# A decoder layer's expert stage: order of the last blocks, place of a token's two expert rows, and who weighs the last two tiles

## The reference

```python
x = hidden_states.reshape(-1, H)                      # 1024 tokens, H = 256
logits = jnp.einsum('th,eh->te', x, gate_w)           # 16 experts
topk_w, topk_idx = jax.lax.top_k(_softmax(logits), 2)
combine = jnp.sum(jax.nn.one_hot(topk_idx, E) * topk_w[..., None], axis=1)
gu = jnp.einsum('th,ehj->etj', x, w_gate_up)          # I = 176, gate and up
y = jnp.einsum('eti,eih,te->th', _swiglu(gu, I), w_down, combine)
y = y + _swiglu(x @ shared_gate_up, 2 * I) @ shared_down
```

## Time and profile before

| | us |
|---|---|
| median of 3 runs | 245.59 (244.62 to 246.39) |
| profiled execution, device time | 245.34 |
| its span | 243.5 |
| around the span | 1.84 |
| TensorE busy in it | 223.9 (92%) |
| VectorE / ScalarE / GpSimd busy | 144.6 / 123.3 / 77.1 |

### The profile page before, as it was taken

How to read it: one execution, slowest core, us unless ns; L and a number is a source line. 1 busy time by engine, 2 the same in 40 slices (tenths; PEclk the granted TensorE clock), 3 DMA queues, 4 the chain that set the end, 5 groups by cost and what they waited for, 6 DMA issues and landing times.

```text
span 243.5 us, 5429 instructions
## 1 busy us (share of the span) xinstructions
PE 223.9 (92%) x1800; PEld 156.7 (64%) x1800; DVE 144.6 (59%) x442; ACT 123.3 (51%) x444; POOL 77.1 (32%) x95
## 2 busy tenths in 40 slices
PE   8978899999999999999999999999999999998970
PEld 6535566656666676889778788776555556554540
DVE  1568878888878878343989468955222322222175
ACT  2136988989898888923242520702333334333310
POOL 2221121111121101020474100274577777752330
PEclk9999999999999999999999999999999999999996
DMA  6999977500001900001502200032595323655596
GB/s 214 264 347 349 316 172 168 133 13 1 1 3 31 307 5 0 4 0 25 215 0 76 99 0 0 5 79 58 146 287 203 108 92 99 155 164 183 178 287 242
DMA packets 21662, 30.62 MB, mean 126 GB/s; under 512 B 2361, under 2 KB 17347, under 8 KB 21635
## 3 DMA queue, kind: packets, MB, share of 16 engines
q1 hardware_dynamic: 18627, 23.34, 32.5%
q0 software_dynamic: 2304, 6.29, 8.7%
q10 hardware_dynamic: 704, 0.64, 0.8%
HBM read 25.02 MB, written 5.24 MB: 124 GB/s over the span
## 4 chain that ended last, share of the span: by engine, by line
PE 56%; ACT 14%; DVE 11%; DMA 8%; issue 5%; SPq 2%; POOL 2%; DVEq 0%; ACTq 0%; POOLq 0%
PE bank L948 11%; ACT pr_s L1073 10%; PE bank L965 7%; PE bank L873 5%; PE bank L575 5%; PE bank L617 4%; PE bank L604 3%; DMA x_s<-expert_out 3%; PE bank L702 3%; PE bank L937 2%; PE bank L927 2%; DMA bxT<-in_wh_t 2%; PE bank L580 2%; PE bank L667 2%; DMA early<-in_w_gu 1%
## 5 line engine op out<-in xcount | busy, mean ns | idle before, releaser
L1073 ACT ACTIVATE pr_s<-bank,mx 128x128 f32<-128x128 f32 x128 | 45.2, 384 | 8.0 <-DVE mx L1302 8.0
L1635 DVE COPY bxT<-bank 128x256 f32<-128x256 f32 x24 | 10.1, 423 | 41.3 <-PE bank L950 38.7
L948 PE MATMUL bank<-gu_s,bxT 128*64 x96 | 31.3, 466 | 1.4 <-DMA early<-in_w_gu 1.4
L536 POOL DMA_INDIRECT expert_out<-by,prT x24 | 23.7, 987 | 17.6 <-ACT by L1063 13.6
L1063 ACT ACTIVATE prT<-bank 128x512 f32<-128x512 f32 (+1 forms) x56 | 27.4, 514 | 2.7 <-PE bank L617 1.8
L1073 ACT ACTIVATION_READ_ACCUMULATOR pr_s<-bank,mx 128x1 f32 x128 | 28.7, 224 | 0.0
L531 POOL DMA_INDIRECT qx_s<-ffn_in,prT x24 | 23.4, 976 | 16.5 <-issue 8.9
L1302 DVE TENSOR_REDUCE mx<-bank 128x4 f32<-128x512 f32 x32 | 20.5, 683 | 4.7 <-PE bank L604 4.7
L965 PE MATMUL bank<-dn_s,prT 88*64 x96 | 22.7, 379 | 0.4 <-ACT prT L1063 0.4
L617 PE MATMUL bank<-tab,pr_s 128*128 128x128 f32 x128 | 19.5, 275 | 3.1 <-ACT pr_s L1073 2.7
L873 PE MATMUL bank<-ck_s,sgu_s 128*128 128x256 f32 (+1 forms) x96 | 22.3, 382 | 0.0
(11 more groups left out here) (203 smaller groups left out, 474.1 us busy)
## 6 DMA issues: line engine op xcount, KB each, us to landing
gu_s<-in_w_gu SPq DMA_DIRECT2D x8, 704.0 KB, 7.3
dn_s<-in_w_dn SPq DMA_DIRECT2D x4, 704.0 KB
early<-in_w_gu SPq DMA_DIRECT2D x8, 352.0 KB, 5.0
early<-in_w_dn SPq DMA_DIRECT2D x8, 176.0 KB
gu_s<-in_ctx_in SPq DMA_DIRECT2D x2, 512.0 KB, 9.6
ffn_in<-x_s SPq DMA_DIRECT2D x4, 256.0 KB, 2.2
cv_s<-expert_out SPq DMA_DIRECT2D x4, 256.0 KB, 3.7
x_s<-expert_out SPq DMA_DIRECT2D x4, 256.0 KB, 5.5
```

The costliest lines, as they stand in the source:

```text
L536: pool.indirect_dma_start(expert_out[:], bass.IndirectOffsetOnAxis(ap=idx[:, 1, k:k + 1], axis=0), by[:, k % RB, :], None).then_inc(dma_sc ...
L948: mm(bank[2 + i % 2][0:HT, 0:2 * I], bxT[:, i % 2, k, 0:HT], gu_s[:, k, bass.ds(e, 1), :], start=k == 0, stop=k == KD - 1, skip_group_chec ...
L1073: last = nc.scalar.activation(pr_s[:, n % 2, h, :], score_bank(n)[:, h * T:(h + 1) * T], ACT.Exp, bias=mx[:, n % 4, h:h + 1], accum_out=de ...
```

## The change

Five edits in one version:

1. A token's two rows of `expert_out` lie side by side: row 2 x token + (0 for the best expert, 1 for the second). The index formula has the same number of operations. The reload reads `(b p k) d`, one piece of 2 KB per partition.
2. TensorE's order: `shared_up(3, 1)` moves from behind block 1's up to behind block 20's down. The loop ends at i = 20 without block 21's up; after it come hidden transpose 20, up 21, down 20, `shared_up(3, 1)`, hidden transpose 21, up 22, up 23, down 21, `shared_up(3, 2)`, hidden transposes 22 and 23, down 22, down 23. ScalarE and VectorE follow the same order. The wait of the first two `expert_down` on the last pair's c = 1 goes; block 1's waits on c = 0. Banks of c = 1 and 2 of the last pair are 6 and 7 in place of 4 and 6.
3. SP's staging order: up 0, up 1, down 0, down 1, up 2, up 3, then (up 4, up 5, down 2, down 3), (up 6, up 7, down 4, down 5), down 6, down 7 (numbers are blocks less 16); waits as before.
4. VectorE makes four diagonal 128 x 128 matrices of the weights of tiles 6 and 7 (`diagonals`, `dg`), and TensorE adds diagonal x rows to the shared expert's result in PSUM (4 matmuls of 128 x 256) once tile 6's, then tile 7's reload has landed. VectorE's `weigh_pair(6)` (4 operations) is gone; its last two additions stay.
5. VectorE does `shared_add(1)` and `shared_add(2)` ahead of `bT_out(0)`.

The diff, with its few constant declarations left out:

```diff
@@ -106,7 +106,7 @@
     c[:, R_RING + RB:R_RING + 2 * RB] = 2 * E + 2 * (RB - 1 - np.arange(RB))
-    c[:, R_DUMMY:R_DUMMY + BLOCKS] = DUMMY + T * np.arange(BLOCKS) + p + 1
+    c[:, R_DUMMY:R_DUMMY + BLOCKS] = DUMMY + T * np.arange(BLOCKS) + p + 2
     return c
@@ -197,6 +197,7 @@
         staged = early[0][:, 0:SB * (KD * 2 * I + 2 * D)].rearrange("p (r n) -> p r n", r=SB)
+        dg = early[0][:, SB * (KD * 2 * I + 2 * D):][:, 0:4 * T].rearrange("p (b k t) -> p b k t", b=2, k=2)
         gu_x = staged[:, :, 0:KD * 2 * I].rearrange("p r (k n) -> p r k n", k=KD)
@@ -336,7 +338,7 @@
         bei = sb("bei", [1, MORE], i32)
-        shared_bank = lambda q, c: bank[((6, 7, 1) if q < PAIRS - 1 else (5, 4, 6))[c]]
+        shared_bank = lambda q, c: bank[((6, 7, 1) if q < PAIRS - 1 else (5, 6, 7))[c]]
         hidden_bank = lambda i: bank[(1, 0)[i % 2]]
@@ -419,21 +421,34 @@
             sp.wait_ge(pe_expert_up, RB)
-            for j in range(BLOCKS - E):
-                e = staged_expert[j]
+            def stage_up(j):
                 if j >= SB:
                     sp.wait_ge(pe_expert_up, E + j - SB + 1)
-                sp.dma_start(gu_x[:, j % SB], w_gu[bass.ds(e, 1), :, :, :].rearrange("e p k n -> p (e k) n")).then_inc(dma_staged_up[j % SB], 16)
+                sp.dma_start(gu_x[:, j % SB], w_gu[bass.ds(staged_expert[j], 1), :, :, :].rearrange("e p k n -> p (e k) n")).then_inc(dma_staged_up[j % SB], 16)
+
+            def stage_down(j):
                 if j >= SB:
                     sp.wait_ge(pe_expert_down, E + j - SB + 1)
-                sp.dma_start(dn_x[:, j % SB], w_dn[bass.ds(e, 1), :, :, :].rearrange("e p k n -> p (e k) n")).then_inc(dma_staged_down[j % SB], 16)
+                sp.dma_start(dn_x[:, j % SB], w_dn[bass.ds(staged_expert[j], 1), :, :, :].rearrange("e p k n -> p (e k) n")).then_inc(dma_staged_down[j % SB], 16)
+
+            for j in range(0, BLOCKS - E, 2):
+                stage_up(j)
+                stage_up(j + 1)
+                if j >= SB:
+                    stage_down(j - 2)
+                    stage_down(j - 1)
+                elif j == 0:
+                    stage_down(0)
+                    stage_down(1)
+            stage_down(BLOCKS - E - 2)
+            stage_down(BLOCKS - E - 1)
             sp.wait_ge(dve_ring, 1)
...
             for t in range(B):
-                sp.dma_start(yg[t],
-                             expert_out[0:SLOTS, :].rearrange("(k b p) d -> b p k d", k=2, b=B)[t]).then_inc(dma_token_outputs[t], 16)
+                sp.dma_start(yg[t].rearrange("p k d -> p (k d)"),
+                             expert_out[0:SLOTS, :].rearrange("(b p k) d -> b p (k d)", k=2, b=B)[t]).then_inc(dma_token_outputs[t], 16)
             for t in range(B - 2):
@@ -957,8 +972,8 @@
                     pe.wait_ge(act_expert_out, i - 1)
-                if i < 2:
-                    pe.wait_ge(dve_shared_hidden, SC * (PAIRS - 1) + 2)
+                if i == 1:
+                    pe.wait_ge(dve_shared_hidden, SC * (PAIRS - 1) + 1)
                 if i >= E:
@@ -1026,38 +1041,47 @@
             expert_up(1)
-            shared_up(PAIRS - 1, 1)
             block_transpose(2)
             block_transpose(3)
-            for i in range(2, BLOCKS, 2):
+            last = BLOCKS - 1
+            for i in range(2, BLOCKS - 2, 2):
                 hidden_transpose(i - 2)
                 hidden_transpose(i - 1)
-                if i + 2 < BLOCKS:
-                    block_transpose(i + 2)
-                    block_transpose(i + 3)
+                block_transpose(i + 2)
+                block_transpose(i + 3)
                 expert_up(i)
-                if i + 2 < BLOCKS:
+                if i + 4 < BLOCKS:
                     expert_up(i + 1)
...
                 expert_down(i - 1)
-                if i + 2 < BLOCKS:
-                    read_expert(i + 2)
-                    read_expert(i + 3)
-                else:
-                    expert_up(i + 1)
+                read_expert(i + 2)
+                read_expert(i + 3)
+            hidden_transpose(last - 3)
+            expert_up(last - 2)
+            expert_down(last - 3)
+            pe.wait_ge(dve_block_T, last)
+            shared_up(PAIRS - 1, 1)
+            hidden_transpose(last - 2)
+            expert_up(last - 1)
+            expert_up(last)
+            expert_down(last - 2)
             shared_up(PAIRS - 1, 2)
-            hidden_transpose(BLOCKS - 2)
-            hidden_transpose(BLOCKS - 1)
-            expert_down(BLOCKS - 2)
-            expert_down(BLOCKS - 1)
+            hidden_transpose(last - 1)
+            hidden_transpose(last)
+            expert_down(last - 1)
+            expert_down(last)
             for c in range(SC):
...
                 for b in range(2):
-                    last = mm(last_pair_out(b), shT[0:r, (PAIRS - 1) % 2, c, b * T:(b + 1) * T], sdn_s[0:r, c, :],
-                              start=c == 0, stop=c == SC - 1)
-                    if c == SC - 1:
-                        last.then_inc(pe_shared_down, 1)
+                    mm(last_pair_out(b), shT[0:r, (PAIRS - 1) % 2, c, b * T:(b + 1) * T], sdn_s[0:r, c, :],
+                       start=c == 0, stop=False)
+            pe.wait_ge(dve_diagonals, 1)
+            for b in range(2):
+                pe.wait_ge(dma_token_outputs[B - 2 + b], 16)
+                for k in range(2):
+                    last = mm(last_pair_out(b), dg[:, b, k, :], yg[B - 2 + b][:, k, :], start=False, stop=k == 1)
+                last.then_inc(pe_shared_down, 1)
         @block.scalar
@@ -1242,21 +1266,28 @@
             silu(1)
-            shared_silu(PAIRS - 1, 1)
-            for i in range(2, BLOCKS, 2):
+            last = BLOCKS - 1
+            for i in range(2, BLOCKS - 2, 2):
                 hT_out(i - 2)
...
                 silu(i)
-                if i + 2 < BLOCKS:
+                if i + 4 < BLOCKS:
                     silu(i + 1)
...
                 y_out(i - 1)
-            silu(BLOCKS - 1)
+            hT_out(last - 3)
+            silu(last - 2)
+            y_out(last - 3)
+            shared_silu(PAIRS - 1, 1)
+            hT_out(last - 2)
+            silu(last - 1)
+            silu(last)
+            y_out(last - 2)
             shared_silu(PAIRS - 1, 2)
-            hT_out(BLOCKS - 2)
-            hT_out(BLOCKS - 1)
-            y_out(BLOCKS - 2)
-            y_out(BLOCKS - 1)
+            hT_out(last - 1)
+            hT_out(last)
+            y_out(last - 1)
+            y_out(last)
             act.wait_ge(dve_shared_added, PAIRS + 1)
@@ -1566,7 +1597,7 @@
                 link(V.reciprocal(top_w[0], s8[:, 6, :]))
-                link(V.tensor_tensor(top_w[1], second_exp, top_w[0], ALU.mult))
+                V.tensor_tensor(top_w[1], second_exp, top_w[0], ALU.mult).then_inc(dve_weights, 1)
@@ -1608,12 +1639,12 @@
             link(V.tensor_tensor(ids[:, 1, :], best_n, ids[:, 0, :], ALU.add))
-            link(V.tensor_scalar(ids[:, 2, :], ids[:, 0, :], 0.0, float(B * T), ALU.is_gt, ALU.mult))
+            link(V.tensor_scalar(ids[:, 2, :], ids[:, 0, :], 0.0, -2.0, ALU.is_gt, ALU.add))
             V.tensor_scalar(idx[:, 0, :], ids[:, 1, :], -1.0, 0.0, ALU.add, ALU.max)
...
             link(V.tensor_tensor(ids[:, 3, :], ids[:, 3, :], ids[:, 2, :], ALU.add))
-            V.scalar_tensor_tensor(idx[:, 1, :], ids[:, 3, :], -1.0, ids[:, 1, :], ALU.add, ALU.add).then_inc(dve_rows, 1)
+            V.scalar_tensor_tensor(idx[:, 1, :], ids[:, 1, :], 2.0, ids[:, 3, :], ALU.mult, ALU.add).then_inc(dve_rows, 1)
             shared_mul(2, 2)
@@ -1648,33 +1679,43 @@
+            def diagonals():
+                dve.wait_ge(dve_weights, 1)
+                for b in range(2):
+                    for k in range(2):
+                        last = V.tensor_scalar_mul(dg[:, b, k, :], idf, top_w[k][:, B - 2 + b:B - 1 + b])
+                last.then_inc(dve_diagonals, 1)
+
+            shared_add(1)
+            shared_add(2)
             bT_out(0)
-            shared_add(1)
             bT_out(1)
...
             h_mul(1)
-            shared_add(2)
-            shared_mul(PAIRS - 1, 1)
             bT_out(2)
...
             router_weights()
-            for i in range(2, BLOCKS, 2):
-                if i + 2 < BLOCKS:
-                    bT_out(i + 2)
+            diagonals()
+            last = BLOCKS - 1
+            for i in range(2, BLOCKS - 2, 2):
+                bT_out(i + 2)
                 h_mul(i)
-                if i + 2 < BLOCKS:
+                if i + 4 < BLOCKS:
                     bT_out(i + 3)
-                h_mul(i + 1)
+                    h_mul(i + 1)
+            h_mul(last - 2)
+            bT_out(last)
+            shared_mul(PAIRS - 1, 1)
+            h_mul(last - 1)
+            h_mul(last)
             shared_mul(PAIRS - 1, 2)
...
             weigh_pair(4)
-            weigh_pair(6)
             for b in range(2):
...
                 dve.wait_ge(pe_shared_down, PAIRS + b)
```

(4 more changed lines are left out.)

## The result

The changed kernel takes 242.38 us in the median of four runs (242.22 to 242.47), where the kernel before took 245.92 in four (244.62 to 246.39; the 245.59 of the table above is the median of three of them): a ratio of 0.9864, with a 95% interval of 0.9824 to 0.9904. It is faster by 1.4%, not by the 2.2% forecast. The profiled execution took 242.47 us with a span of 240.6, so 1.87 us lie around it (1.84 before); the forecast had a span of 238.05. The missing 2.5 us are all at the end, as the rows show from the front on.

A forecast was written before the change was run, and what follows sets the result against it. Bound: TensorE's program up to block 20's down, then the reloads. Last addition at 235.8, plus 2.25 gives span 238.05 (5.45 us less); 1.84 around it and 0.25 for the median give 240.1 us, range 238.6 to 242.4.

The forecast's parts named there:

- the front's gain: Loop front: without `shared_up(3, 1)` there, block 2's up begins at 168.1 to 168.4, taken as 2.0 us earlier.
- the stall for staged weights: TensorE before block 21's up: SP's new order removes the wait, a gain of 1.56 us (ends 0 and 1.56).
- block 20's down and the reloads: Loop end: block 20's down begins at 220.13 instead of 225.21, so the reloads begin at 224.28, 5.1 us earlier.
- The cover that was named: Idle time or room said to hide the `shared_add`, the making of four diagonals and the reloads' landing, each costed at nothing.
- The four diagonal matmuls are 128 x 256 like the twelve, 2.86 / 12 = 0.24 each: 0.96: TensorE's end: the diagonal products add 0.96 us, so TensorE ends at 235.1.
- 2.25 us on, the span ends: Program end: the last addition ends at 235.8 and the span 2.25 us later, at 238.05.
- rival A: Program end: a transfer, scatter 23's landing or the last stores, sets the end; span 238.7, time 240.8; chance 0.13.
- a hold of one weighing: Within rival A: a scatter's issue on GpSimd might be held by one two-input VectorE weighing, 0.5 us.
- B: Loop end: the staging stall only moves, to block 20's or 22's weights; up to 1.56 us, time 241.7; chance 0.11.
- C: Loop front: the gain is not had, a gather or something hidden holds it; 2.0 us, time 242.1; chance 0.07.
- D: Block loop: scatters of interleaved rows land late and hold `y_out`; slower, up to 248.8 us; chance 0.03.
- E: Reloads: 2 KB pieces do not shorten the landing; changes nothing in the time, no chance of its own.

The follow-up runs named there:

- three diagonals: Changed kernel with waits before weighings 6, 7, 9 and 10, and tile 6's best row weighed on VectorE again, leaving three diagonal products: 240.20 us, ratio 0.9796.
- four gaps: Changed kernel with only weighings 6, 7, 9 and 10 waiting for the one before: ratio 0.9842 on the second chip; 240.55 us, ratio 0.9807 on the third.

## Why the prediction was right and where it failed

**Right.** What bound the kernel before, and every step up to the first weighing: the front's gain of 2.0 us (168.30 in the trace), the stall for staged weights gone, block 20's down and the reloads 5.0 us sooner, each within 0.13 us. The cover that was named hid what it should: `shared_add` and the diagonals cost nothing, and the reloads of tiles 6 and 7 landed at 232.7 and 234.4, before the products of tile 6, at 234.07, and of tile 7, at about 235.0, wanted them. All this holds for the first result and the third chip; on the second the front's gain did not reach the reloads.

**Failed, the term "The four diagonal matmuls are 128 x 256 like the twelve, 2.86 / 12 = 0.24 each: 0.96".** The mechanism was right, the size half. A float32 product with 128 columns of weights leaves two records, and the "twelve" of the earlier trace rows are six instructions (three chunks, two tiles), as the eight of a `shared_up` are four; the unit should have been 0.48 us for an instruction. The products took 1.89 us, and the weighings were quicker than summed (4.8 us, not 5.6, since back to back they come every 0.40 us). Together the last addition ended 0.6 us later than forecast. The run with three diagonals confirms the term.

**Failed, the step "2.25 us on, the span ends", and with it the price of rival A.** The forecast took the stretch from the last addition to the end from the trace of before. Rival A named the scatter of block 23 as what might set the end instead, and that is what happened, but not by its landing, which took 2.5 us: by its issue, 3.0 us late. The forecast weighed a hold of one weighing, 0.5 us, and dismissed it because one scatter beside weighings had taken 0.97 us. That one had a gap of 0.11 us to get in by, and the next, of 1.05 us, was passed over. The change itself took the gaps away: with every reload landed before its own weighing is due (tile 3's at 230.5 for the sixth weighing at 231.4, tile 5's at 232.1 for the tenth at 233.0), VectorE has nothing to wait for, and the twelve weighings form one unbroken row. The held scatter took 3.85 us, and GpSimd's drain, which ended at 242.3 in the kernel before, 1 us ahead of SP, became the last. With the hold taken away alone (four gaps, third chip) the span is 238.6 us, 0.55 above the forecast of 238.05, and the last addition, at 236.35, is late by the same 0.55, which is the diagonals' part.

The page "SBUF — State Buffer" of the Trainium skill, section Who interferes with whom, says that a VectorE instruction with two SBUF inputs contends with a GpSimd instruction that reads SBUF, and that one with a single SBUF input, outside the two-port modes, does not. The runs agree with both halves: 3.85 us with two, 0.97 with one from PSUM. In its bullet on the two-port modes the page has the other engine blocked for a whole instruction. Two scatters here were held for one weighing, 1.10 and 1.19 us; the scatters of four runs were held for the whole row, 3.85 and 5.44 us.

**Luck.** The measured 242.38 us lies just inside the stated range of 238.6 to 242.4. That is chance: the upper end was there for rivals such as B and C, which did not come in this run, and the hold of 1.9 us stood in no term.

**Rivals B, C and D** did not come in the first result: no wait before block 20's down, block 2's up on time, and ScalarE waited for a scatter only once, for 1.5 us, off the path. On the first two chips of the experiments ScalarE's copies wait 19 to 28 us for an unrecorded release in every kernel traced, also with the rows in their old place. **E** was right in its effect as far as the runs can tell: the kernel before with 2 KB pieces has the ratio 0.999.

## What to carry to other kernels

A helper engine off the critical path may need gaps in its neighbour's work, and a change that packs the neighbour's instructions without gaps can starve it; when weighing such a hold, take the length of the unbroken row as its upper end, not that of one instruction. Test a change on more than one chip before its parts are priced: what binds the loop may differ. Where the end of a program moves forward, look at every engine's closing instruction, not at the last store alone, since one that ended shortly before may be next. Count matmuls as instructions, from the code, before taking a price from records.

## What the hardware showed that was not expected

- VectorE's weighings back to back start every 0.40 us though each lasts 0.47. Beside such a row with two SBUF operands a GpSimd scatter took 3.85 us (twelve weighings, three runs) and 5.44 (sixteen), where it takes 0.97 alone or with one operand in PSUM, and 1.06 to 1.13 with gaps. In two short rows it took 1.10 and 1.19 without a gap. A semaphore wait on the weighing before makes a gap of 0.04 us and costs 0.14 (6.3 against 4.8 us for eleven of them).
- GpSimd's closing drain ended 2.0 to 2.5 us after its last scatter had landed, in the six traces that record the landing (240.35 and 242.36 in the kernel before, 237.9 and 240.4 in the changed one). So where that scatter is late, the span waits for the drain and not for the landing.
- With the same program, two blocks took 5.3 us in the first result and on the third chip, and 6.2 on the two other chips, where ScalarE's copies wait for a release that the trace does not record. It stays open why.
